# Layer two's low-rank down term: row groups of v added on DVE, two closing products a tile instead of six

## The reference

```python
def lora(x, W, A, B, idx):            # idx: the sample's adapter
    base = einsum('bsd,df->bsf', x, W)
    return base + einsum('bsr,brf->bsf', einsum('bsd,bdr->bsr', x, A[idx]), B[idx])   # rank 16
gate = lora(x, Wg, Ag, Bg, idx)       # 256 -> 1024
up   = lora(x, Wu, Au, Bu, idx)       # 256 -> 1024
h    = silu(gate) * up
y    = lora(h, Wd, Ad, Bd, idx)       # 1024 -> 256
x    = x + (y @ (weight * scale).T + bias)      # folded by the kernel into Wd and Bd
```

## Time and profile before

| | us |
|---|---|
| median of 3 runs (606.17 to 607.83) | 607.19 |
| the profiled execution, its own time | 604.36 |
| its span, first to last instruction | 602.6 |
| PE busy | 574.8 (95%) |
| DVE busy | 358.6 (60%) |
| ACT busy | 241.7 (40%) |
| POOL busy | 148.9 (25%) |

### The profile page before, as it was taken

How to read it: one execution, slowest core, us unless ns; L and a number is a source line. 1 busy time by engine, 2 the same in 40 slices (tenths; PEclk the granted TensorE clock), 3 DMA queues, 4 the chain that set the end, 5 groups by cost and what they waited for, 6 DMA issues and landing times.

```text
span 602.6 us, 10239 instructions
## 1 busy us (share of the span) xinstructions
PE 574.8 (95%) x3576; PEld 479.6 (80%) x3576; DVE 358.6 (60%) x807; ACT 241.7 (40%) x545; POOL 148.9 (25%) x127
## 2 busy tenths in 40 slices
PE   4767899999999999999999999999999999999996
PEld 2646699999999999988878878878788788788784
DVE  7888767874785666766544554455455455544533
ACT  2644357666865755553412312414124123124010
POOL 3000224753462460756003022040040040100000
PEclk9998899999999999999999999999999999999998
DMA  8998568362357330733005014042041050130012
GB/s 319 344 318 254 182 235 287 54 178 52 36 144 260 36 62 9 193 62 97 0 0 147 12 66 90 3 120 39 0 139 17 0 146 11 52 68 6 11 26 35
DMA packets 64989, 61.97 MB, mean 103 GB/s; under 512 B 37616, under 2 KB 56816, under 8 KB 63600
## 3 DMA queue, kind: packets, MB, share of 16 engines
q1 hardware_dynamic: 53168, 37.99, 21.0%
q0 software_dynamic: 9600, 23.14, 15.8%
q10 hardware_dynamic: 2176, 0.26, 0.3%
HBM read 46.10 MB, written 19.47 MB: 109 GB/s over the span
## 4 chain that ended last, share of the span: by engine, by line
PE 89%; DVE 6%; DMA 1%; SPq 1%; ACT 1%; issue 1%; DVEq 0%
PE bank L1258 25%; PE bank L1259 24%; PE bank L1260 24%; PE bank L1503 5%; PE bank L1461 2%; DMA xT<-in_xT 1%; DVE passed L885 1%; PE bank L1315 1%; PE bank L1330 1%; PE bank L1368 1%; PE bank L1453 1%; PE bank L1359 1%; PE bank L1470 1%; PE bank L1471 1%; SPq L393 1%; PE bank L1591 1%
## 5 line engine op out<-in xcount | busy, mean ns | idle before, releaser
L728 ACT ACTIVATE act<-bank 128x512 f32<-128x512 f32 x64 | 38.2, 598 | 189.5 <-PE bank L1503 189.5
L1215 DVE TENSOR_TENSOR prod<-bank,act 128x512 f32<-128x512 f32 x64 | 44.2, 691 | 98.5 <-PE bank L1503 97.6
L1094 DVE TENSOR_TENSOR hid_lo<-hf,hid_hi 128x512 fp32r<-128x512 f32 (+1 forms) x80 | 46.7, 585 | 50.6 <-ACT hf L658 50.3
L1258 PE MATMUL bank<-w_hi,hid_hi 128*128 128x256 f32 x256 | 71.8, 280 | 0.0
L1259 PE MATMUL bank<-w_lo,hid_hi 128*128 128x256 f32 x256 | 71.4, 279 | 0.0
L1260 PE MATMUL bank<-w_hi,hid_lo 128*128 128x256 f32 x256 | 71.3, 279 | 0.0
L655 ACT ACTIVATE hid_hi<-bank 128x512 fp32r<-128x512 f32 (+1 forms) x80 | 41.1, 514 | 65.1 <-PE bank L1260 64.7
L487 POOL DMA_INDIRECT x_rows<-y_sb,slot_row x32 | 54.4, 1699 | 43.7 <-ACT y_sb L627 32.6
L476 POOL DMA_INDIRECT xg<-flat_rows,slot_row x32 | 34.6, 1082 | 118.9 <-DVE slot_row L951 74.6
L1258 PE MATMUL bank<-xs_hi,w_hi 128*128 128x512 f32 (+1 forms) x160 | 57.1, 357 | 0.5 <-DVE xs_lo L961 0.5
L506 POOL DMA_INDIRECT b_pair<-b_rows,b_row x8 | 8.0, 1004 | 197.5 <-PE bank L1552 196.8
(11 more groups left out here) (295 smaller groups left out, 1271.0 us busy)
## 6 DMA issues: line engine op xcount, KB each, us to landing
w_raw<-in_L_ffn_W SPq DMA_DIRECT2D x8, 1024.0 KB, 7.2
flat_rows<-x_sb SPq DMA_DIRECT2D x8, 520.0 KB, 7.5
xT<-in_xT SPq DMA_DIRECT2D x8, 512.0 KB, 7.9
x_sb<-in_x SPq DMA_DIRECT2D x8, 512.0 KB, 8.6
outT<-out_sb SPq DMA_DIRECT2D x120, 32.0 KB, 1.6
wdT<-in_wdT SPq DMA_DIRECT2D x1, 1024.0 KB, 5.9
wg_lo_raw<-in_L_cond_Wg SPq DMA_DIRECT2D x1, 1024.0 KB, 8.3
wu_lo_raw<-in_L_cond_Wu SPq DMA_DIRECT2D x1, 1024.0 KB, 4.9
```

What stands on the lines that cost most here:

```text
L728: act.activation(act1[h % 2][:, :], bank[h % 2][:, :], ACT.Silu).then_inc(silu1, 1)
L1094: dve.tensor_tensor(lo[:, n], hf[s % 2][:, n], hi[:, n].bitcast(f32), ALU.subtract).then_inc(hid0, 1)
L1215: dve.tensor_tensor(prod[par][h][:, :], bank[2 + h % 2][:, :], act1[h % 2][:, :], ALU.mult).then_inc(prod1, 1)
L1258: pe.matmul(out, lh, rh, start=start, stop=False, skip_group_check=True)
```

## The change

- v's four row groups are added up on DVE: a copy of row group 0 out of bank 6 into `v_sum`, and three additions, each of one row group of the bank with what `v_sum` has so far, each writing one row group further on. The masking then takes 32 rows (0 to 31) only.
- The masked v is rounded into rows 0 to 31 of `vm_hi`, again into rows 64 to 95, and its low part goes to rows 32 to 63. Rows 96 to 127 are set to zero once, by a `memset` ahead of `first_uu`.
- The gathered Bd has high rows in rows 0 to 63 and low rows in 64 to 127 (new column 8 of `cols`), so one product over 128 rows gives all three split terms. `finish` has two products, one for each k. One gather a tile instead of two.
- `low_rank_down` moves from step 1, ahead of `down1_`, to step 0, behind `down1_`.
- Tile 7 closes as before (`finish_last_v`, two gathers). One more 128-row DVE instruction on 7 or 8 numbers in `pair_rows`.

```diff
-F2_COLS = {"cols": 8, "iota": P, ...
+F2_COLS = {"cols": 9, "iota": P, ...
...
-                          p % RANK + P * (p // 32 == 1), p % RANK, p % RANK + P], 1).astype(np.float32),
+                          p % RANK + P * (p // 32 == 1), p % RANK, p % RANK + P,
+                          p % RANK + P * (p // 64)], 1).astype(np.float32),
...
-        vs = sb("vs", [P, BT], f32r)
+        vs, v_sum = sb("vs", [P, BT], f32r), sb("v_sum", [P, BT], f32)
...
+        v_add, v_zero = sem("v_add"), sem("v_zero")
...
             def gather_bd(t):
                 if t >= 2:
                     pool.wait_ge(acc1, t - 1)
-                for i in range(2):
+                for i in range(2 if t == NB1 - 1 else 1):
...
+                dve.tensor_scalar(bd_row[:, 0, 0:NB1 - 1], b_row_f[:, 1, 0:NB1 - 1], float(RANK), cols[:, 8:9], ALU.mult, ALU.add)
                 for i in range(2):
-                    last = dve.tensor_scalar(bd_row[:, i, :], b_row_f[:, 1, :], float(RANK), cols[:, 6 + i:7 + i], ALU.mult, ALU.add)
+                    last = dve.tensor_scalar(bd_row[:, i, NB1 - 1:], b_row_f[:, 1, NB1 - 1:], float(RANK), cols[:, 6 + i:7 + i],
+                                             ALU.mult, ALU.add)
...
             def finish_v(t):
+
                 dve.wait_ge(v_mm, t + 1)
-                masked(vm, bank[6], t).then_inc(v_ev, 1)
+                dve.tensor_copy(v_sum[32:64, :], bank[6][0:32, :]).then_inc(v_add, 1)
+                for i in range(1, 4):
+                    r, to = slice(32 * i, 32 * i + 32), slice(32 * i + 32, 32 * i + 64) if i < 3 else slice(0, 32)
+                    dve.wait_ge(v_add, 4 * t + i)
+                    dve.tensor_tensor(v_sum[to, :], bank[6][r, :], v_sum[r, :], ALU.add).then_inc(v_add, 1)
+                dve.wait_ge(v_add, 4 * t + 4)
+                masked(vm, v_sum, t, slice(0, 32)).then_inc(v_ev, 1)
                 dve.wait_ge(v_ev, t + 1)
+                dve.tensor_copy(vm_hi[0:32, :], vm[0:32, :]).then_inc(v_hi, 1)
+                dve.tensor_copy(vm_hi[64:96, :], vm[0:32, :])
+                dve.wait_ge(v_hi, t + 1)
+                dve.tensor_tensor(vm_hi[32:64, :], vm[0:32, :], vm_hi[0:32, :].bitcast(f32), ALU.subtract).then_inc(v_lo, 1)
+
+            def finish_last_v():
+
+                dve.wait_ge(v_mm, NB1)
+                masked(vm, bank[6], NB1 - 1).then_inc(v_ev, 1)
+                dve.wait_ge(v_ev, NB1)
                 dve.tensor_copy(vm_hi[:, :], vm[:, :]).then_inc(v_hi, 1)
-                dve.wait_ge(v_hi, t + 1)
+                dve.wait_ge(v_hi, NB1)
                 dve.tensor_tensor(vs[:, :], vm[:, :], vm_hi[:, :].bitcast(f32), ALU.subtract).then_inc(v_lo, 1)
...
             u_masked(0)
+            dve.memset(vm_hi[96:128, :].bitcast(f32), 0.0).then_inc(v_zero, 1)
             first_uu()
...
             def finish(t, par, pair):
 
+                if isinstance(t, int) and t == 0:
+                    pe.wait_ge(v_zero, 1)
                 pe.wait_ge(v_lo, t + 1)
-                pe.wait_ge(bd_in[par], 32 * (pair + 1))
+                pe.wait_ge(bd_in[par], 16 * (pair + 1))
                 for k in range(KD):
-                    bd_hi, bd_lo = (bd_pair[par][:, i, k * P:(k + 1) * P] for i in range(2))
-                    pe.matmul(bank[4 + k][:, :], bd_hi, vm_hi[:, :], start=False, stop=False, skip_group_check=True)
-                    pe.matmul(bank[4 + k][:, :], bd_lo, vm_hi[:, :], start=False, stop=False, skip_group_check=True)
-                    last = pe.matmul(bank[4 + k][:, :], bd_hi, vs[:, :], start=False, stop=True, skip_group_check=True)
+                    last = pe.matmul(bank[4 + k][:, :], bd_pair[par][:, 0, k * P:(k + 1) * P], vm_hi[:, :], start=False, stop=True,
+                                     skip_group_check=True)
                 last.then_inc(acc1, 1)
...
                     pair_half(par, pair, 1, uu[par], bank[2 + h % 2], h, up1, t)
-                    if h == 1 and not first:
-                        low_rank_down(t - 1, 1 - par, range(KH))
...
                     elif not first:
                         down1_(s - 2, KH - 2 + h, t - 1, 1 - par, first)
+                    if h == 0 and not first:
+                        low_rank_down(t - 1, 1 - par, range(KH))
```

More of the change, by code:

```diff
@@ L35 @@
 F_COLS = {"ident": P, "adapter": NAD, "gate_w": KD * 32, "subj_w": NAD * 32}
-F2_COLS = {"cols": 8, "iota": P, "before": P, "restart": 2 * E * G, "behind": E * G, "gate_b": E,
+F2_COLS = {"cols": 9, "iota": P, "before": P, "restart": 2 * E * G, "behind": E * G, "gate_b": E,
            "scale": D, "out_bias": KD}
@@ L1138, in _, with masked @@
                         last_lo(q)
[L1140 to L1144, removed]
+            def masked(dst, src, t, r=slice(None)):
+                m = adapter_mask[r, bass.ds(t * SB, SB)]
+                return dve.tensor_tensor(dst[r, :].rearrange("p (s n) -> p s n", n=32),
+                                         src[r, :].rearrange("p (s n) -> p s n", n=32), over(m, 32), ALU.mult)
             def x1_low(par, n, k, src):
@@ L1248, in _ @@
             steps1(NB1 - 1, 1, NB1 // 2 - 1, False, True)
-            finish_v(NB1 - 1)
+            finish_last_v()
             finish_last(16 * SB * (NB1 // 2 - 1))
@@ L1534, in finish_last @@
                 pe.wait_ge(v_lo, NB1)
-                pe.wait_ge(bd_in[par], 32 * (NB1 // 2))
+                pe.wait_ge(bd_in[par], 16 * (NB1 // 2 - 1) + 32)
                 for k in range(KD):
```

## The result

Four runs of the changed kernel: 600.31 us median (599.81 to 601.47), against 607.51 (606.17 to 609.08) for the kernel before in four runs. The ratio of the runs is 0.9898, with a 95% interval of 0.9867 to 0.9929: 6.2 us off, between 4.3 and 8.1 (the medians alone lie 7.2 apart). Forecast were 602.1 us in 600.0 to 605.2, so 5.1 off; the median lies only 0.3 above the low end of that range.

A forecast was written before the change was run, and what follows sets the result against it. PE was taken to set the time in layer two. 6.5 us for removed products, less 1.0 at the down products and 0.45 for the memset, gave 5.1 us off 607.19: 602.1 us, range 600.0 to 605.2.

The forecast's parts named there:

- PE is the bound, and four products are 0.93 us a tile: Layer two: PE sets the time; two closing products for six gain 0.93 us in tiles 0 to 6, 6.5 in all.
- The move costs nothing: `low_rank_down` behind step 0's down products: own cost unchanged, no added wait, copy starts 3.3 us sooner than the mask did.
- DVE's chain: `finish_v`, 3 to 8 instructions: from the copy, subtraction ends at 5.35 to 5.49 us, 0.7 ahead of the closing products.
- The quadrant rule: DVE: output starting in another 32-partition group waits for all earlier instructions, so `prod` follows the subtraction by 0.71 us, not 0.61.
- The row at 270.56: Profile row of the kernel before, on DVE, cited for a distance of 0.71 us from subtraction to `prod`.
- The loss at the down products: Tile's first down products wait for `finish_out`: 0 to 0.31 us a loop closing, 0.20 taken; 1.0 us over all seven.
- 0.14 for the hand-over: From the end of a DVE instruction to the start of the PE product waiting for it: 0.14 us.
- The slow follower: On PE, the product after one that had to wait comes 0.31 us behind instead of 0.23: 0.08 each.
- all hidden: Rival: DVE spacings at their short ends, no closing costs over 0.05 us; 6.05 us gained, 601.1 us; chance 0.28.
- The memset: On DVE between `u_masked(0)` and `first_uu`, all paid: 0.45 us taken, bounds 0.17 and 0.69.
- The sum: Whole kernel: 6.5 - 1.0 - 0.45 = 5.05, 5.1 us off, giving 602.1 us.
- The slower rival: DVE's chain becomes the bound, PSUM reads into another row group costing double: 8.7 us slower, 615.8 us; chance 0.05.

The follow-up runs named there:

- the runs above: The changed kernel with one more 32-row addition in DVE's chain ahead of the masking: 602.51 us against 605.23; with two more: 608.48 us against 606.87.
- the repeat: The changed kernel once more, with no further change, beside runs of the kernel before: 599.36 us against 605.23, ratio 0.9908.

## Why the prediction was right, point by point

**PE is the bound, and four products are 0.93 us a tile.** Right to the hundredth: 41.55 became 40.62, and with six products again it was 41.55. Seven closings give 6.5, read as a whole between the first and the last block.

**The move costs nothing.** Right (ratio 1.0003 alone), and it is what makes the change possible: without it the kernel is 19 us slower than the one before.

**DVE's chain.** The copy was put at 2.31 behind the last product, and came 2.31 behind it (429.59 to 431.90). The end of the subtraction was put at 5.35 to 5.49 and came at 5.27, `finish_out` at 7.15 to 7.49 and came at 7.19 in this loop tile (6.98 to 6.99 outside the loop, 0.2 earlier where 0.14 was forecast). Its parts were right or slightly long: the second cast took 0.42, with no slow one, and the additions 0.69. The quadrant rule of the Trainium skill (VectorE: DVE Perf Modes, section Two Vector instructions with no wait between them) held: `prod` came 0.71 behind the subtraction and not 0.61. The row at 270.56, from which the forecast took the 0.71, is no case of a changed output group: by the kernel both subtractions there write rows 64 to 95, and it is the inputs that move from rows 0 to rows 32. The clean case came with the runs above. The one added instruction and the mask behind it both write rows 0 to 31 and stand 0.61 apart; the two added ones read the same rows, write 0 to 31 and 32 to 63, and they and the mask (0 to 31) stand 0.70 and 0.69 apart.

**The loss at the down products is the step that failed.** It was a term of 1.0 us in all, and measured 0. The size that was too large is the chain's: the term was taken from the late half of its range (first out instruction ending at 7.90 to 8.24), and the chip came at the early end, 7.93. With the forecast's own 0.14 for the hand-over that is 8.07, and PE comes to this product at 8.23, also counted from the copy: already hidden. The 0.14 was sound as an upper value. Behind the subtraction the runs show 0.05 to 0.14 (in the old place 449.53 + 0.68 to 450.35), behind the out instruction 0.05 or 0.15. The slow follower is real (0.31 to 0.34 behind instead of 0.23), but it is only paid by a product that waits. The rival "all hidden" is what happened in the tiles, with a chance of 0.28.

**The memset.** 0.45 was forecast, and it costs 0.63. The instruction takes 0.48, as the slope gave; the 0.16 of idle time ahead of it was not in the sum.

**The sum.** By the rows, 6.5 - 0.63 is 5.9. Timed against runs of before: 6.2 at first (4.3 to 8.1), 5.6 in the repeat (4.1 to 7.1). The rows lie in both intervals; the forecast of 5.1 was 0.8 short: 1.0 from the term above, less the 0.18 that the memset cost beyond 0.45. That the measured time still lies in the range is in part owed to how its low end was drawn: at "all hidden", and 0.9 us further for scatter.

**The slower rival.** Its mechanism is real: two additions more end at +1.6 us, the old place at +19. Its point was put at 0.86 us lost at a closing, which two instructions more (1.1 to 1.25 lost) pass. Its premise, additions that cost double for reading PSUM into another row group, is false: 0.69 each.

**"Minimize op *count*"**, the rule of the Trainium skill (VectorE: DVE Perf Modes, section Rules for kernel authors), mattered here only where DVE was late: five more at each closing cost nothing, a sixth 3 us in all.

## What to carry to other kernels

Where one engine is never idle, taking work off it is worth the distance between its instructions, to the hundredth, even if another engine gets over three times that much to do; but write out the other engine's chain up to the last wait that hangs on it (here not the closing product but the down product that overwrites its bank 2 us later), and buy slack by starting that chain earlier, at no cost, before lengthening it. A one-time initialisation belongs in a pause, ahead of the work that waits for another engine and not behind it. And judge such a change by the distance of one recurring instruction, which repeats to 0.03 us where the whole run scatters by 2.

## What the runs showed of the hardware that I had not expected

PE gaps of 2.1 to 2.3 us in otherwise full work were followed by the lower clock level in five of seven closings (products 0.43 us apart for about 3 us), and not in the other two, behind gaps as long (`low_rank_down` in its old place). Short gaps can so cost half as much again as they last.

A product released by a wait starts 0.05 to 0.15 us after DVE's instruction has ended. The same two instructions give either value in different tiles, so the kind of instruction doesn't decide it; what does, these runs don't show. Its follower stands 0.31 (behind 0.15) or 0.34 (behind 0.05) after it instead of 0.23.

An instruction put between two dependent ones on DVE is partly free in the loop. There the third addition and the mask start 0.85 us apart, outside it 0.72. With one more addition between them both are 1.33 apart: 0.48 more in the loop, 0.61 outside it. So 0.13 us of the register work for the mask's offset went under the added instruction.
